# LSTM stage of a fused kernel: input rows added into the gate banks by TensorE, h split into three bf16 columns, no filler products

## The chip, the cores and the metric

The kernel runs on one core of a Trainium2 chip. The metric is the device time of one execution in microseconds (us), the median of three runs. TensorE is called PE, VectorE DVE, ScalarE ACT, GpSimd POOL and the DMA-issuing SyncE SP.

## The reference

The reference is a chain of eight layers over 625 rows of 512 features. Each adds its output to the rows. The change concerns the sixth, a recurrent cell chosen anew at each of 625 steps among four LSTM cells:

```python
def step(carry, x_t):
    h, c = carry
    logits = concatenate([h, c, x_t]) @ W_sel.T + b_sel
    onehot = one_hot(argmax(logits), 4)
    g_all = x_t @ W_ih[s] + h @ W_hh[s] + b_ih + b_hh        # for each cell s
    i, f, g, o = split(sum over s of g_all * onehot, 4)
    c2 = sigmoid(f) * c + sigmoid(i) * tanh(g)
    h2 = sigmoid(o) * tanh(c2)
    return (h2, c2), h2
```

Step 0 starts from c = 0 and uses cell 0. h, c and each gate have 512 elements. The 625 values of h are added to the rows.

## The kernel before

Eight stages run one after the other, each in blocks that end when every engine has ended. The function lstm has four such blocks, and the changed lines are all in them, save the host's layout of the constants (lay_out).

**lstm_inputs** (L1125) computes the input product of all steps and all four cells ahead of the recurrence. 64 tiles, one for each cell and each 128 of its 2,048 gate rows, take 4 f32 products (K = 128 each) of 313 and of 312 columns (L1218, L1220). ACT and DVE add the bias as they copy the tile out of PSUM (L1204, L1189), and POOL's queue stores 5 MB for each cell (L1174).

**split_weights** (L1257) loads the recurrent weights (4 loads of 4 MB), finds a power of two from their largest value, and writes each weight, times that scale, as two fp16 parts.

**lstm_steps** (L1334) is the recurrence: a loop on each engine, 624 times round. A state vector of 512 lies as 128 partitions of 4 columns. The order of one round is:

- PE adds the score of the four cells in one PSUM row: the input's part (L1434), c's part (L1437, 8 narrow f32 records), and tanh(c) against weights that were multiplied by the output gate (L1441, 8 records).
- DVE takes the largest score and its index (MAX8 L1524, FIND_INDEX8 L1526). PE reads the index into a register and branches to one of four bodies. DVE reads it too, and copies the input row of that step and cell out of a ring (L1530).
- The body, cell(s), has 96 products (L1456). h, as two fp16 columns (high part, rest) of a 128x32 stationary tile, is the operand that is loaded; the fp16 weights stream past it. Four products stand side by side in the array's columns (tile_position 0, 32, 64, 96). They come in three parts, each in its own PSUM bank: f (32 products of 128 columns), i and g together (32 of 256), o (32 of 128).
- DVE sums the 32 rows of each bank (add_rows, L1480), multiplies by the inverse scale and adds the input (add_input, L1486), and ACT applies sigmoid or tanh (L1406 to L1413). DVE makes f*c (L1492), i*g (L1497), c (L1503), the weighted score weights (L1507), h (L1513), h's high part (L1516) and h's rest (L1518). ACT makes tanh(c) (L1415). POOL copies h away (L1396).
- keep_clock_up (L1424) issues products of 128x128 by 512 columns into a bank that nobody reads: 3 after the score, 1 when h's rest is there, 4 after the body (L1427).

SP loads the ring of input rows, 25 steps at a time (L1379 to L1389).

**add_hidden** (L1572) turns the kept h and adds it to the rows.

Of the kernel before, what the change touches and what calls it, by code (L numbers as in the profile page):

```python
# [24 lines left out]
WARM_PICK, WARM_GATES = 4, 4  # L25
H_SCALE = 1024.0
# [1093 lines left out]
CHUNK = 25  # L1120
RING = 3 * CHUNK

def lstm_inputs(nc, ctx, B):  # L1125
# [7 lines left out]
    def sem(name):  # L1133
        return nc.alloc_semaphore("xg_" + name)

    (b_loaded, bias_ready, done, kept_a, kept_v, lx_done, lx_kept, lx_stored) = [sem(n) for n in (
        "b_loaded bias_ready done kept_a kept_v lx_done lx_kept lx_stored").split()]
    w_loaded = [sem(f"w_loaded{i}") for i in range(2)]
    stored = [sem(f"stored{i}") for i in range(2)]
    B.xg = nc.dram_tensor("lstm_xg", (CELLS, 128, STEPS * GC), F32, kind="Internal").ap()  # L1140
    B.lx = nc.dram_tensor("lstm_lx", (STEPS, CELLS), F32, kind="Internal").ap()
    xnT = B.xnT[:].rearrange("p (c n) -> p c n", c=KC)
    CUT = 313
    LOADS = 2 * CELLS
    with ExitStack() as here:
        w = sb("w", [128, 2, KC, GC // 2, 128], F32)
        b_ih = sb("b_ih", [128, CELLS * GC], F32)
        b_hh = sb("b_hh", [128, CELLS * GC], F32)
        ws = sb("ws", [128, KC, CELLS], F32)
        bs = sb("bs", [1, CELLS], F32)  # L1150
        g = sb("g", [128, 2, STEPS, GC], F32)
# [3 lines left out]
        @block.sync  # L1155
        def _(sp):
            sp.dma_start(b_ih[:], I["c_b_ih"]).then_inc(b_loaded, 16)
            sp.dma_start(b_hh[:], I["c_b_hh"]).then_inc(b_loaded, 16)
            sp.dma_start(ws[:], I["c_w_sel_x"]).then_inc(b_loaded, 16)
            sp.dma_start(bs[:], I["L2_ffn_b_sel"].rearrange("(a s) -> a s", a=1)).then_inc(b_loaded, 16)  # L1160
            for n in range(LOADS):
                if n >= 2:
                    sp.wait_ge(done, GC // 2 * (n - 1))
                sp.dma_start(w[:, n % 2], I["c_w_ih"][n // 2, :, :, n % 2]).then_inc(w_loaded[n % 2], 16)
            sp.wait_ge(lx_kept, 1)
            sp.dma_start(B.lx.rearrange("(j p) s -> p j s", p=R), lx[:]).then_inc(lx_stored, 16)
            sp.wait_ge(lx_stored, 16)

        @block.gpsimd
        def _(pool):  # L1170
            for s in range(CELLS):
                pool.wait_ge(kept_a, GC * (s + 1))
                pool.wait_ge(kept_v, GC * (s + 1))
                pool.dma_start(B.xg[s], g[:, s % 2].rearrange("p t g -> p (t g)")).then_inc(stored[s % 2], 16)  # L1174
            for i in range(2):
                pool.wait_ge(stored[i], 16 * (CELLS // 2))

        @block.vector
        def _(dve):
            dve.wait_ge(b_loaded, 64)  # L1180
            nc.vector.tensor_tensor(b_ih[:], b_ih[:], b_hh[:], ALU.add).then_inc(bias_ready, 1)
            dve.wait_ge(bias_ready, 1)
            for s in range(CELLS):
                if s >= 2:
                    dve.wait_ge(stored[s % 2], 16 * (s // 2))
                for c in range(GC):
                    i = s * GC + c
                    dve.wait_ge(done, i + 1)
                    nc.vector.tensor_scalar(g[:, s % 2, CUT:STEPS, c], B.bank[2 * (i % 4) + 1][:, 0:STEPS - CUT],  # L1189
                                            b_ih[:, i:i + 1], None, ALU.add).then_inc(kept_v, 1)  # L1190
            dve.wait_ge(lx_done, 1)
            nc.vector.tensor_copy(lx[:], B.bank[0][0:R, 0:NT * CELLS].rearrange("p (j s) -> p j s", j=NT)
                                  ).then_inc(lx_kept, 1)

        @block.scalar
        def _(act):
            act.wait_ge(bias_ready, 1)
            for s in range(CELLS):
                if s >= 2:
                    act.wait_ge(stored[s % 2], 16 * (s // 2))  # L1200
                for c in range(GC):
                    i = s * GC + c
                    act.wait_ge(done, i + 1)
                    nc.scalar.activation(g[:, s % 2, 0:CUT, c], B.bank[2 * (i % 4)][:, 0:CUT], ACT.Identity,  # L1204
                                         bias=b_ih[:, i:i + 1]).then_inc(kept_a, 1)

        @block.tensor
        def _(pe):
            for i in range(CELLS * GC):
                n = i // (GC // 2)  # L1210
                if i % (GC // 2) == 0:
                    pe.wait_ge(w_loaded[n % 2], 16 * (n // 2 + 1))
                if i >= 4:
                    pe.wait_ge(kept_a, i - 3)
                    pe.wait_ge(kept_v, i - 3)
                for c in range(KC):
                    wt = w[:, n % 2, c, i % (GC // 2), :]
                    nc.tensor.matmul(B.bank[2 * (i % 4)][:, 0:CUT], wt, xnT[:, c, 0:CUT], start=(c == 0),  # L1218
                                     stop=(c == KC - 1))
                    last = nc.tensor.matmul(B.bank[2 * (i % 4) + 1][:, 0:N - CUT], wt, xnT[:, c, CUT:N],  # L1220
                                            start=(c == 0), stop=(c == KC - 1))
                last.then_inc(done, 1)
            pe.wait_ge(b_loaded, 64)
            pe.wait_ge(kept_a, CELLS * GC)
            pe.wait_ge(kept_v, CELLS * GC)
            for m in range(NT):
                o = B.bank[0][0:R, m * CELLS:(m + 1) * CELLS]
# [11 lines left out]
def lstm(nc, ctx, B):  # L1239

    lstm_inputs(nc, ctx, B)
    with ExitStack() as here:
# [4 lines left out]
        L.raw = sb("w", [128, BLOCKS + SHIFT, 512], F32)  # L1247
        L.inv = sb("inv_scale", [128, 1], F32)
# [1069 lines left out]
```

## Time and profile before

| | |
|---|---|
| median of 3 runs | 6274.82 us (6270.7 to 6276.47) |
| the profiled execution | 6278.15 us |
| its span, first to last instruction | 6276.3 us |
| granted TensorE clock, mean of the span | 0.944 of full speed |
| PE busy | 5392.8 us (86%) |
| DVE busy | 3097.9 us (49%) |
| ACT busy | 1088.6 us (17%) |
| the recurrence's rounds | 2307.7 to about 5536 us |

Busy time of PE is modelled: a product of 512 fp16 columns counts some 0.38 us, of which the next one overlaps a part. A granted clock of 1.00 is 2.4 GHz, 0.50 is 1.2 GHz.

### The profile page before, as it was taken

The numbers are of one execution on the slowest core, as the hardware profiler recorded it, in microseconds if no ns is written. First come the engines' busy times: TensorE is split into PE (matmuls) and PEld (weight loads), VectorE is DVE, ScalarE is ACT, GpSimd is POOL, SyncE is SP. The second block draws the span as 40 slices with busy tenths as digits, with TensorE's granted clock in tenths as the row PEclk, the third lists the DMA queues.
The fourth block names the chain that finished last, engine by engine and source line by source line (L and its number), as shares of the span: only waits on it lengthen the run. The fifth ranks groups of instructions, "written<-read, shape, count | busy, mean of one in ns | idle before, by whom it ended". The sixth has DMA issues, their size and how long they took to land. (4 is left out here: it accounts for less than half of the span.)

```text
span 6276.3 us, 214043 instructions
## 1 busy us (share of the span) xinstructions
PE 5392.8 (86%) x84948; PEld 3269.5 (52%) x84948; DVE 3097.9 (49%) x13265; ACT 1088.6 (17%) x4645; POOL 612.9 (10%) x1014
## 2 busy tenths in 40 slices
PE   8998778849998929999999999999999999977778
PEld 6643443314666615555555555555555555544444
DVE  4401443214552165555555555555555555564543
ACT  0000000002331131111111111111111111122312
POOL 0000660002650000000000000000000000011100
PEclk9999998979999969999999999999999999989877
DMA  0000111467432330000000000000000000000010
GB/s 10 21 30 11 39 44 44 97 136 253 119 105 100 139 123 5 5 5 10 5 5 5 10 5 5 5 5 10 5 5 5 5 10 0 0 24 37 23 55 9
DMA packets 128787, 240.28 MB, mean 38 GB/s; under 512 B 47084, under 2 KB 64114, under 8 KB 127687
## 3 DMA queue, kind: packets, MB, share of 16 engines
q1 hardware_dynamic: 68584, 146.72, 6.6%
q0 software_dynamic: 60128, 92.58, 5.9%
q8 instruction: 45, 0.74, 0.0%
q14 instruction: 30, 0.25, 0.0%
HBM read 165.58 MB, written 73.29 MB: 38 GB/s over the span
## 5 line engine op out<-in xcount | busy, mean ns | idle before, releaser
L1456 PE MATMUL bank<-lstm_w,step_h_parts 128*32 128x128 f16 (+1 forms) x59904 | 1233.0, 238 | 172.1 <-issue 164.0
L1456 PEld LDWEIGHTS bank<-lstm_w,step_h_parts 128*32 128x32 f16 x59904 | 1116.8, 97 | 488.4 <-issue 478.0
L1427 PE MATMUL bank<-lstm_w 128*128 128x512 f16 x4992 | 1297.0, 383 | 3.2 <-issue 3.2
L1480 DVE TRANSPOSE_TENSOR_REDUCE step_summed<-bank 128x4 f32<-128x128 f32 x1872 | 670.0, 358 | 292.7 <-PE bank L1456 285.6
L1427 PEld LDWEIGHTS bank<-lstm_w 128*128 128x128 f16 x4992 | 386.4, 98 | 388.5 <-issue 5.1
L1406 ACT ACTIVATE step_act_out<-step_gates 128x4 f32<-128x4 f32 x625 | 128.5, 206 | 2082.3 <-DVE step_gates L1486 2078.8
L1486 DVE SCALAR_TENSOR_TENSOR step_gates<-step_summed,lstm_inv_scale,step_xgs 128x4 f32<-128x4 f32 x1872 | 416.0, 222 | 68.7
L1530 DVE COPY step_xgs<-step_xg 128x16 f32 x624 | 109.2, 175 | 688.7 <-issue 664.5
L1396 POOL COPY xnT<-step_state 128x4 f32 (+1 forms) x625 | 116.4, 186 | 3170.0 <-DVE step_state L1513 3170.0
L1109 PE MATMUL bank<-sum_parts,sum_hot 125*125 125x512 f16 x1600 | 347.6, 381 | 6.9 <-DVE sum_parts L1068 6.9
L1437 PE MATMUL bank<-lstm_wsel,step_state 128*1 128x4 f32 x4992 | 214.9, 168 | 115.3 <-DVE step_state L1503 115.3
L1109 PEld LDWEIGHTS bank<-sum_parts,sum_hot 125*125 125x125 f16 x1600 | 219.7, 137 | 135.1 <-DVE sum_parts L1068 7.8
L539 POOL DMA_INDIRECT gcn_rows<-gcn_h_rows,gcn_idx x160 | 202.5, 1266 | 704.4 <-issue 704.4
L1434 PEld LDWEIGHTS bank<-step_input_score,ones 1*1 1x1 f32 x1248 | 50.8, 76 | 380.4 <-issue 380.4
L1437 PEld LDWEIGHTS bank<-lstm_wsel,step_state 128*1 128x1 f32 x4992 | 147.1, 81 | 181.7 <-DVE step_state L1503 181.6
L227 PE MATMUL bank<-cnt_hot_s,cnt_hot_d 125*125 125x512 bf16 x800 | 222.2, 388 | 3.4 <-DVE cnt_hot_s L203 3.4
L1010 POOL DMA_INDIRECT sum_rows<-rel_h,sum_idx x160 | 212.1, 1326 | 118.3 <-DVE sum_idx L1063 80.3
L617 PE MATMUL bank<-gcn_hot,gcn_rows 125*128 125x500 f32 x320 | 177.9, 638 | 46.9 <-DMA gcn_rows<-gcn_h_rows,gcn_idx 43.0
L1434 PE MATMUL bank<-step_input_score,ones 1*1 1x4 f32 x1248 | 116.6, 161 | 115.9 <-ACT step_input_score L1411 115.9
L1441 PE MATMUL bank<-step_h_weight,step_tc 128*1 128x4 f32 x4992 | 214.2, 168 | 0.0
L944 PE MATMUL bank<-rel_zg,rel_mix 128*128 128x512 f32 x312 | 136.0, 599 | 76.8 <-DMA rel_z_last<-rel_z 76.8
L1218 PE MATMUL bank<-xnT,xg_w 128*128 128x313 f32 x512 | 178.2, 429 | 10.4 <-DMA xg_w<-in_c_w_ih 10.4
(368 smaller groups left out, 6578.2 us busy)
## 6 DMA issues: line engine op xcount, KB each, us to landing
rel_h<-rel_h_sb SPq DMA_DIRECT2D x39, 1024.0 KB, 4.3
lstm_xg<-xg_g POOLq DMA_DIRECT2D x4, 5000.0 KB, 19.5
step_xg<-lstm_xg SPq DMA_DIRECT2D x25, 800.0 KB, 4.4
xg_w<-in_c_w_ih SPq DMA_DIRECT2D x8, 2048.0 KB, 10.7
lstm_w<-in_c_w_hh SPq DMA_DIRECT2D x4, 4096.0 KB, 30.8
rel_z<-rel_z_sb POOLq DMA_DIRECT2D x8, 1250.0 KB, 22.9
rel_zg<-rel_z POOLq DMA_DIRECT2D x8, 1248.0 KB
cheb_w<-in_L_gnn_weight SPq DMA_DIRECT2D x8, 1024.0 KB
```

Of the source, the lines that this page charges most:

```text
L227: nc.tensor.matmul(B.bank[m][0:R, :], hd, hot_s[:, b, 0:512], start=False, stop=False)
L539: nc.gpsimd.indirect_dma_start(out=rows[:, i, :], out_offset=None, in_=h_dram, in_offset=bass.IndirectOffsetOnAxis(ap=idx[:, i:i + 1], axis=0)
L617: nc.tensor.matmul(B.bank[0][0:H, 0:500], rows[:, i, :], hot[:, i % 2, 0:500], start=False, stop=False)
L1010: nc.gpsimd.indirect_dma_start(out=rows[:, i, :], out_offset=None, in_=B.rel_h, in_offset=bass.IndirectOffsetOnAxis(ap=idx[:, i:i + 1], ax ...
L1109: last = nc.tensor.matmul(B.bank[m][0:R, :], hot[:, i % BUFS, m * R:(m + 1) * R], parts[:, i % BUFS, a, :], start=False, stop=False)
L1218: nc.tensor.matmul(B.bank[2 * (i % 4)][:, 0:CUT], wt, xnT[:, c, 0:CUT], start=(c == 0), stop=(c == KC - 1))
L1427: nc.tensor.matmul(idle[:], w[:, 0, 0, 0, 0, 0:128], w[:, 0, 0, 0, 0, :], start=True, stop=True)
L1437: nc.tensor.matmul(score[:, 0:CELLS], state[:, k:k + 1], L.wsel[:, :, k], start=False, stop=False)
L1441: last = nc.tensor.matmul(score[:, 0:CELLS], tc[:, k:k + 1], h_weight[:, :, k], start=False, stop=(k == KC - 1))
L1456: last = nc.tensor.matmul(bank[32 * q:32 * q + 32, 0:32 * (end - first)], h_parts[:, c, :], w[:, s, c, q, a, 32 * first:32 * end], start=( ...
L1480: nc.vector.tensor_reduce(summed[:, first:end], bank[:, 0:32 * (end - first)].rearrange("p (b r) -> p b r", r=32), X_AXIS, ALU.add, apply_ ...
L1486: nc.vector.scalar_tensor_tensor(out=gates[:, first:end], in0=summed[:, first:end], scalar=L.inv[:, 0:1], in1=xgs[:, first:end], op0=ALU.mult,
```

## The change

In the recurrence, the input rows are no longer copied and added by DVE. They lie in SBUF as bf16 rows: for each of the 16 pairs of gate and quarter three parts (high, middle, low), in 48 partitions, and the bias in another 48. One product for each gate (inject) with a constant 0/1 matrix as the loaded operand puts the rows of all four cells, 512 columns, into that gate's bank; the body then adds the recurrent product onto the 128 columns of the chosen cell. The gates are four parts now (f, g, i, o), each of 32 products of 128 columns. Injections of f and g stand at the head of PE's round, those of i and o after the score; keep_clock_up is gone. h is multiplied by the weights' inverse scale (a value in memory, in place of the constant 1024) and split in three bf16 columns; the split's second half (three DVE instructions) stands behind the choice of the cell. The add_input instructions are gone, and ACT reads the sums. lstm_inputs computes 80 tiles of 125 rows by 512 columns, splits them in three bf16 parts on ACT and DVE, and stores each tile by itself. The ring holds 15 steps in loads of 5.

```diff
@@ lstm_inputs
-                    nc.scalar.activation(g[:, s % 2, 0:CUT, c], B.bank[2 * (i % 4)][:, 0:CUT], ACT.Identity,
-                                         bias=b_ih[:, i:i + 1]).then_inc(kept_a, 1)
+                nc.scalar.copy(parts[:, i % 8, 0], B.bank[i % 6][0:R, :]).then_inc(hi_ready, 1)
+                nc.vector.tensor_tensor(rest[:, i % 4], B.bank[i % 6][0:R, :], parts[:, i % 8, 0], ALU.subtract
+                                        ).then_inc(rest_ready, 1)
+                nc.scalar.copy(parts[:, i % 8, 1], rest[:, i % 4]).then_inc(mid_ready, 1)
+                nc.vector.tensor_tensor(parts[:, i % 8, 2], rest[:, i % 4], parts[:, i % 8, 1], ALU.subtract
+                                        ).then_inc(lo_ready, 1)
+            for i in range(TILES):
+                n, m = i // NT, i % NT
+                pool.wait_ge(lo_ready, i + 1)
+                pool.dma_start(B.xg[n, :, m * R:(m + 1) * R, :].rearrange("a t g -> t a g"), parts[:, i % 8]
+                               ).then_inc(stored[i % 8], 16)
@@ lstm_steps, sync
+            sp.wait_ge(cleared, 1)
+            sp.dma_start(xg[64:64 + XG_ROWS, :, :], bias_rows.to_broadcast((XG_ROWS, XG_RING, 512))
+                         ).then_inc(bias_loaded, 16)
+                sp.wait_ge(injected, (k - (XG_SLOTS - 1)) * XG_CHUNK - 1)
+                load(k, k % XG_SLOTS)
@@ lstm_steps, tensor
-            def keep_clock_up(products):
-
-                for _ in range(products):
-                    nc.tensor.matmul(idle[:], w[:, 0, 0, 0, 0, 0:128], w[:, 0, 0, 0, 0, :], start=True, stop=True)
+            def inject(part, at, stop):
+                p, bank, _, _ = part
+                return nc.tensor.matmul(bank[:], rows[:, p, :], xg[:, at, :], start=True, stop=stop)
+
+            def add_half(part, s, c, a, stop):
+                p, bank, _, _ = part
+                for q in range(4):
+                    last = nc.tensor.matmul(bank[32 * q:32 * q + 32, 128 * s:128 * s + 128], h_parts[:, c, :],
+                                            w[:, s, c, q, a, 128 * p:128 * p + 128], start=False, stop=stop,
+                                            tile_position=(0, 32 * q))
+                return last
+
+            def cell(s):
+                for part in parts:
+                    for c, a in halves:
+                        last = add_half(part, s, c, a, stop=(c == KC - 1 and a == 1))
+                    last.then_inc(part[2], 1)
             with pe.Fori(1, STEPS) as t:
 
-                pe.wait_ge(init, 1)
-                pe.wait_ge(input_score_ready, t)
+                pe.wait_ge(xg_loaded, (t // XG_CHUNK + 1) * 16)
+                at = bass.ds(t % XG_RING, 1)
+                for part in (part_f, part_g):
+                    pe.wait_ge(part[3], t)
+                    inject(part, at, stop=False)
+                pe.wait_ge(input_score_ready, 1)
+                pe.sem_inc(input_score_ready, -1)
...
                 last.then_inc(score_done, 1)
-                keep_clock_up(WARM_PICK - 1)
-                pe.wait_ge(init, 1)
+                for part in (part_i, part_o):
+                    pe.wait_ge(part[3], t)
+                    last = inject(part, at, stop=False)
+                last.then_inc(injected, 1)
+                pe.wait_ge(picked, 1)
                 pe.wait_ge(h_lo_ready, t)
-                keep_clock_up(1)
-                pe.wait_ge(picked, 1)
                 s = pe.value_load(pick[0:1, 0:1])
...
-                keep_clock_up(WARM_GATES)
@@ lstm_steps, vector
-            def add_input(part, t):
+            def add_rows(part, s, n):
+                p, bank, done, summed_part = part
+                nc.vector.tensor_reduce(summed[:, 4 * p:4 * p + 4], bank[:, bass.ds(s * 128, 128)].rearrange(
+                    "p (b r) -> p b r", r=32), X_AXIS, ALU.add, apply_transpose=True
+                                        )._wait_ge(done, 1).then_inc(summed_part, 1)
...
-                nc.vector.scalar_tensor_tensor(out=state[:, 4:8], in0=act_out[:, 12:16], scalar=H_SCALE, in1=tc[:],
+                nc.vector.scalar_tensor_tensor(out=state[:, 4:8], in0=act_out[:, 12:16], scalar=L.inv[:, 0:1], in1=tc[:],
                                                op0=ALU.mult, op1=ALU.mult).then_inc(h_ready, 1)
                 dve.wait_ge(h_ready, n)
                 nc.vector.tensor_copy(h_parts[:, :, 0], state[:, 4:8]).then_inc(h_hi_ready, 1)
+
+            def split_h(n):
                 dve.wait_ge(h_hi_ready, n)
-                nc.vector.tensor_tensor(h_parts[:, :, 1], state[:, 4:8], h_parts[:, :, 0], ALU.subtract
+                nc.vector.tensor_tensor(h_rest[:], state[:, 4:8], h_parts[:, :, 0], ALU.subtract).then_inc(h_rest_ready, 1)
+                dve.wait_ge(h_rest_ready, n)
+                nc.vector.tensor_copy(h_parts[:, :, 1], h_rest[:]).then_inc(h_mid_ready, 1)
+                dve.wait_ge(h_mid_ready, n)
+                nc.vector.tensor_tensor(h_parts[:, :, 2], h_rest[:], h_parts[:, :, 1], ALU.subtract
                                         ).then_inc(h_lo_ready, 1)
...
                 nc.vector.max_index(pick[:], top[:], score).then_inc(picked, 1)
+                split_h(t)
                 dve.wait_ge(picked, 1)
                 s = dve.value_load(pick[0:1, 0:1], min_val=0, max_val=CELLS - 1)
-                dve.wait_ge(xg_loaded, (t // CHUNK + 1) * 16)
-                nc.vector.tensor_copy(xgs[:], xg[:, bass.ds(s, 1), bass.ds((t % RING) * GC, GC)]
-                                      ).then_inc(xgs_ready, 1)
                 dve.sem_inc(score_done, -1)
                 dve.sem_inc(top_ready, -1)
+                parts_taken()
+            with dve.Fori(1, STEPS) as t:
+                s = choose(t)
+                finish(s, t, t + 1)
```

parts_taken takes one off each of the four done semaphores. finish runs, in this order, the sums of f and g, f*c, the sums of i and o, i*g, c, the score weights, h and its high part. ACT runs f, g (tanh), i, the copy of the input score, o and tanh(c).

## Rows read from the trace of the kernel before

**Rows 1.** Windows: input block, recurrence. PE PEld DVE ACT POOL busy, PEclk, DMA.

```profile
1893.00:2185.00 292.00, 279.36 (x1066) 202.07 (x1066) 52.37 (x74) 55.08 (x69) 2.25 (x4) 0.97 0.29 113
...
2324.00:5535.00 3211.00, 2924.00 (x75885) 1857.94 (x75884) 1905.23 (x10574) 594.99 (x3732) 115.88 (x622) 1.00 0.02 6
```

**Rows 2.** Source L1524, the index search: duration, first and last start.

```profile
L1524 DVE MAX8 step_top<-bank x620: 160/163/164, 2330.5 to 5526.0; 1x8 f32<-1x8 f32 x155
```

**Rows 3.** Timeline of a round: start, us, instruction, [idle before it].

```profile
3502.39 1.95 PE L1456 MATMUL bank<-lstm_w,step_h_parts 128*32 128x128 f16 x96 [0.15 <-issue]
3502.84 0.17 DVE L1530 COPY step_xgs<-step_xg 128x16 f32 x1 [1.10 <-issue]
3503.41 0.32 DVE L1480 TRANSPOSE_TENSOR_REDUCE step_summed<-bank 128x4 f32<-128x128 f32 x1 [0.40 <-PE bank L1456]
...
3503.98 0.44 DVE L1480 TRANSPOSE_TENSOR_REDUCE step_summed<-bank 128x8 f32<-128x256 f32 x1
...
3504.27 1.04 PE L1427 MATMUL bank<-lstm_w 128*128 128x512 f16 x4
...
3504.60 0.31 DVE L1480 TRANSPOSE_TENSOR_REDUCE step_summed<-bank 128x4 f32<-128x128 f32 x1
...
3505.12 0.16 DVE L1497 TENSOR_TENSOR step_ig<-step_act_out 128x4 f32<-128x4 f32 x1 [0.21 <-ACT step_act_out L1409]
...
3505.41 0.16 DVE L1503 TENSOR_TENSOR step_state<-step_fc,step_ig 128x4 f32<-128x4 f32 x1
...
3505.85 0.16 DVE L1513 SCALAR_TENSOR_TENSOR step_state<-step_act_out,step_tc 128x4 f32<-128x4 f32 x1
...
3505.96 0.34 PE L1441 MATMUL bank<-step_h_weight,step_tc 128*1 128x4 f32 x8
3506.04 0.18 DVE L1516 CAST step_h_parts<-step_state 128x4 f16<-128x4 f32 x1
...
3506.26 0.18 DVE L1518 TENSOR_TENSOR step_h_parts<-step_state,step_h_parts 128x4 f16<-128x4 f32 x1
3506.34 0.16 DVE L1524 MAX8 step_top<-bank 1x8 f32<-1x8 f32 x1
...
3506.61 0.15 DVE L1526 FIND_INDEX8 step_pick<-step_top,bank 1x8 uint32<-1x8 f32 x1
...
3507.57 1.95 PE L1456 MATMUL bank<-lstm_w,step_h_parts 128*32 128x128 f16 x96 [0.30 <-issue]
```

**Rows 4.** Timeline, the last round: body and its first sum.

```profile
5532.63 1.95 PE L1456 MATMUL bank<-lstm_w,step_h_parts 128*32 128x128 f16 x96 [0.29 <-issue]
...
5533.33 0.32 DVE L1480 TRANSPOSE_TENSOR_REDUCE step_summed<-bank 128x4 f32<-128x128 f32 x1 [0.21 <-PE bank L1456]
```

**Rows 5.** Timeline, the first rounds.

```profile
2309.41 2.96 PE L1456 MATMUL bank<-lstm_w,step_h_parts 128*32 128x128 f16 x74
2310.51 0.32 DVE L1480 TRANSPOSE_TENSOR_REDUCE step_summed<-bank 128x4 f32<-128x128 f32 x1 [1.12 <-PE bank L1456]
...
2312.21 0.45 DVE L1480 TRANSPOSE_TENSOR_REDUCE step_summed<-bank 128x8 f32<-128x256 f32 x1 [1.05 <-PE bank L1456]
...
2316.31 1.89 PE L1427 MATMUL bank<-lstm_w 128*128 128x512 f16 x4 [3.24 <-issue]
```

**Rows 6.** Windows where the granted clock changed, columns as in rows 1.

```profile
2312.10:2315.50 3.40, 0.78 (x36) 0.43 (x26) 2.08 (x11) 0.73 (x5) 0.19 (x1) 1.00 0.55 202
2315.50:2319.00 3.50, 2.69 (x23) 1.09 (x24) 0.16 (x1) 0.00 (x0) 0.00 (x0) 0.51 0.02 5
5534.30:5537.70 3.40, 1.98 (x28) 1.18 (x16) 1.96 (x11) 0.67 (x4) 0.19 (x1) 1.00 0.00 0
5537.70:5541.10 3.40, 3.40 (x16) 3.40 (x16) 2.75 (x13) 0.00 (x0) 0.00 (x0) 0.50 0.01 2
```

**Rows 7.** Page, DMA issues: KB each, us to landing.

```profile
lstm_xg<-xg_g POOLq DMA_DIRECT2D x4, 5000.0 KB, 19.5
step_xg<-lstm_xg SPq DMA_DIRECT2D x25, 800.0 KB, 4.4
```

More of the change, by code:

```diff
@@ L1207, in _, with keep_mid @@
+            def keep_mid(i):
+                act.wait_ge(rest_ready, i + 1)
+                nc.scalar.copy(parts[:, i % 8, 1], rest[:, i % 4]).then_inc(mid_ready, 1)
+            for i in range(TILES + 1):
+                if i < TILES:
+                    keep_hi(i)
+                if i >= 1:
+                    keep_mid(i - 1)
         @block.tensor
         def _(pe):
-            for i in range(CELLS * GC):
-                n = i // (GC // 2)
-                if i % (GC // 2) == 0:
+            for i in range(TILES):
+                n, m = i // NT, i % NT
+                if m == 0:
@@ L1247, in lstm @@
         L.raw = sb("w", [128, BLOCKS + SHIFT, 512], F32)
+        L.scale = sb("scale", [128, 1], F32)
         L.inv = sb("inv_scale", [128, 1], F32)
@@ L1359, in lstm_steps @@
+    w = L.raw[:, 0:BLOCKS, :].bitcast(F16).rearrange("p (s c q) (a k) -> p s c q a k", s=CELLS, c=KC, a=2)
+    part_f = (0, B.bank[0], done_f, summed_f)
+    part_g = (1, B.bank[1], done_g, summed_g)
+    part_i = (2, B.bank[2], done_i, summed_i)
+    part_o = (3, B.bank[3], done_o, summed_o)
+    parts = (part_f, part_g, part_i, part_o)
+    score = B.bank[4][0:1, 0:8]
+    halves = [(c, a) for c in range(KC) for a in range(2)]
     with ExitStack() as here:
-        xg = sb("xg", [128, CELLS, RING * GC], F32)
@@ L1555, in _ @@
             dve.wait_ge(init, 1)
-            dve.wait_ge(xg_loaded, 16)
-            for first, end, _, _, _, gates_part in parts:
-                nc.vector.tensor_copy(gates[:, first:end], xg[:, 0, first:end]).then_inc(gates_part, 1)
-            forget(1)
-            new_i(1)
-            new_c(1)
-            weigh_h(1)
-            new_h(1)
-            choose(1)
-            with dve.Fori(1, STEPS - 1) as t:
-                finish(t, t + 1)
-                choose(t + 1)
-            finish(STEPS - 1, STEPS)
+            dve.wait_ge(rows_loaded, 16)
+            nc.vector.tensor_copy(rows[:], rows_f[:]).then_inc(rows_ready, 1)
+            finish(0, None, 1)
+            with dve.Fori(1, STEPS) as t:
+                s = choose(t)
+                finish(s, t, t + 1)
 def add_hidden(nc, ctx, B, L):
@@ L2290, in lay_out @@
         b = out.pop("L2_ffn_" + name).reshape(4, 4, 4, 4, 32)[:, order]
-        out["c_" + name] = np.ascontiguousarray(b.transpose(2, 4, 0, 1, 3).reshape(128, 64))
+        out["c_" + name] = np.ascontiguousarray(b.transpose(1, 2, 0, 3, 4).reshape(16, 512))
+    rows = np.zeros((128, 4, 128), np.float32)
+    for n in range(16):
+        rows[3 * n:3 * n + 3, n // 4, 32 * (n % 4)] = 1.0
+        rows[64 + 3 * n:64 + 3 * n + 3, n // 4, 32 * (n % 4)] = 1.0
+    out["c_xg_rows"] = rows
     w = out.pop("L2_ffn_W_sel")
```

252 lines of the change are left out of this document (125 added, 127 removed).

## The prediction

> **What bounds the kernel now.** I read the windows by stage first. The reader should see that the recurrence fills 3,211 of 6,276 us, that PE is busy 2,924 us of it at a granted clock of 1.00, and that the input block ahead of it is a PE stretch too, 279 of 292 us [rows 1]. The busy 91% is no proof that PE bounds the loop, because a good part of it is keep_clock_up. So the second view is the timeline of one round, read from instruction to instruction. The mean round is (5526.0 - 2330.5) / 619 = 5.16 us [rows 2]; the one that I take apart has 3507.57 - 3502.39 = 5.18 us [rows 3]. Counted from its first body product: the sum of f starts at 1.02, that of i and g at 1.59, that of o at 2.21 and it ends at 2.52; i*g starts at 2.73, c at 3.02 and ends at 3.18; the score's second half starts at 3.57, the largest score at 3.95, and the index is there at 4.37 (3506.61 + 0.15). The next body starts 0.81 later. Each of these waits for the one before it. The round is a chain of latencies over PE, DVE and ACT, and only what is on that chain has a price. The keep_clock_up products (1.04 us for four) start at 1.88, when the body is out, and lie beside the chain.
>
> **The gate part: a gain of 0.52 us a round.** The f sum starts at 1.02 inside the loop, but at 0.70 (5533.33 - 5532.63) in the last round, which stands behind the loop [rows 4]. The difference is DVE's register work: value load, input copy, decrements and loop end. The new loop has its loop end elsewhere, but four more decrements and the split ahead of this sum. From the index on, DVE now needs 3503.41 + 5.18 - 3506.76 = 1.8 us or less to its first sum; the split's dispatch adds some 0.4, and PE's product chain gives 0.60 + 0.81 + 0.70 = 2.1. The two are level; I take 0.70, and up to 1.0 would change nothing, because the o part decides. The body streams the same columns (32 x 128 four times for 32 x 128, 32 x 256, 32 x 128), so its 1.95 us stay. A consumer starts 0.04 after a product's modelled end (5.96 + 0.34 = 6.30, the search at 6.34 [rows 3]). So the o sum starts at 1.99 and ends at 2.30. No add_input and no late sigmoid stand between, since the i sum is finished before 2.0. i*g goes from 2.30 to 2.46, c from 2.50 to 2.66. Before it was 3.18: gain 0.52. Bounds: 0.40 (a semaphore step more) and 0.62 (i*g overlaps the sum's end).
>
> **The head of PE's round: a loss of 0.32.** The injections of f and g now stand ahead of the score on PE's queue, and behind the body, the loop's branch, and register work that PE did not do before (t over 5, t modulo 15, a computed operand address). keep_clock_up's products, which lay over the branch, are gone. No row shows this head. The nearest is DVE's 1.10 us of issue ahead of L1530, which has a value load in it [rows 3]; the bounds are 0 and 1.10, and I take 0.75, nearer to the upper end since the loop's branch is in it. The first injection then starts at 1.88 + 0.75 = 2.63. Four 512-column products take 1.04 us, the last one 0.38 of it by the page's model, so they follow each other at 0.22; two end their streaming at 3.07. The input's and c's score products take some 0.3 more, and the second half starts at 3.37. The chain would have been ready for it at 3.57 - 0.52 = 3.05. The loss is 0.32, with bounds 0 and 0.67. Queued behind the waiting injections is the whole score, and DVE's search waits for that. The injections of i and o come after the score and end 0.44 later, beside the search and the split: they cost nothing at full clock.
>
> **The split: a loss of 0.60.** Before, h's rest was made (6.26) ahead of the search, beside the score products. Now three dependent DVE instructions stand behind the index, and PE reads the index only after the last of them. h, its high part and its rest started 0.19 and 0.22 apart [rows 3], so three take 0.60 (bounds 0.48, three bare durations of 0.16, and 0.66). Everything of the next body is behind it. h with a scale from memory and DVE's loop end, now ahead of the search, cost 0 to 0.1; they hide in the 0.32 above, and cost that much if the head of PE's round is short.
>
> **Sum of the round at full clock:** 5.16 - 0.52 + 0.32 + 0.60 = 5.56 us, or +0.40. By the bounds it is between +0.08 (head hidden; 0.52 and 0.60 kept) and +0.75.
>
> **Around the loop: 0, give or take 10 us.** The input block streams 80 x 4 x 512 = 163,840 columns instead of 64 x 4 x 625 = 160,000: 2.4% of 272 us, +7. Its evictions (two ACT and two DVE passes a tile, in 3.4 us of PE time; now DVE and ACT are busy 52 and 55 of 292 us) and its 80 stores on POOL's queue hide behind PE; without that cover a store costs its landing, which no row shows at this size. The last store is 0.4 MB and not 5 MB (19.5 us to land [rows 7]), the first weight load 1 MB and not 2: some -10. The recurrence begins with a clearing of the ring, a bias load and a ring load in a row instead of a ring load alone (4.4 us [rows 7]): +5. SP issues 125 ring loads of 0.24 MB, each ten rounds (50 us) ahead against 4.4 us to land: nothing.
>
> **The clock: the largest term.** The filler streamed 8 x 0.22 = 1.7 us a round, the injections stream 0.9. Behind a body, PE then has 5.56 - 1.88 = 3.7 us with four injections (by the page's model two pairs of 0.60 = 1.2 us busy) and the four-column score products (some 0.7 busy). What the trace shows near that: in 2312.1 to 2315.5 PE was busy 0.78 of 3.40, and the clock was 0.51 in the next window; in 5534.3 to 5537.7 it was busy 1.98 of 3.40, with the last body's end, the four filler products and the first transposes, and the clock was 0.50 next. [rows 6] In the loop before, with both fillers in each round, it stayed at 1.00 for 3,200 us [rows 1]. I expect it to fall to 0.50 (1.2 GHz) in the stretch behind a body, again and again, and to come back only after a dense stretch, which is a slow body, so that it is high where PE has little to do. The price is in the first rounds: at half clock the sum of i and g started 2312.21 - 2309.41 = 2.80 after the body's start, at full clock 1.59 [rows 3, 5]. That is 1.21 for three quarters of the columns, and 1.61 for all. Four 512-column products take 1.89 instead of 1.04 us, 0.21 more each: 0.42 for the two injections ahead of the score [rows 5]. All at half clock: 5.56 + 1.61 + 0.42 = 7.59. I take two bodies in three and one injection pair in two: 1.07 + 0.21 = 1.28, a round of 6.84.
>
> The Trainium skill (TensorE: Matmul & The Clock Gate, "Why this matters for your kernels") says otherwise: throughput drops come from long PE-idle gaps between bursts of matmuls, and the gap it names is longer than any in this loop. By that rule alone the clock holds and the first rival below would be the result.
>
> **Rivals.**
> - *Forecast, chance 0.60: the clock falls.* 624 x (6.84 - 5.16) = 1,048; on the profiled execution's own 6,278 us that is 7,326, rounded to 7,330. Its own range: 6,800 (bodies at half clock in one round of three, a short head) to 7,800 (624 x 2.43 = 1,516, all at half clock).
> - *The clock holds, 0.27.* For it: the injections are full-width products, two before and two after the score, and the body still comes once a round. Against it: rows 6. 6,278 + 624 x 0.40 = 6,528, between 6,330 (+0.08) and 6,750 (+0.75).
> - *Faster, 0.06.* The place is the stretch from the body's last product to c. If c came over 0.60 us earlier, more than the split costs, with the head of PE's round hidden and the clock up, the kernel would gain; at 0.70 it is 6,278 - 624 x 0.10 = 6,216. For it: the f sum waits 0.3 us for DVE in the loop now. Against: I find 0.52 with the shortest steps of the rows.
> - *No change, 0.02:* the same, with gain and loss level.
> - *Instruction supply, 0.03.* A body is 128 products and loads for 96. In the first rounds PE stood 3.24 us on issue after its first body [rows 5] and never again. If the longer loop brought that back each round: +2,000 us, 8,300.
> - *The input block becomes bound by its stores, 0.02.* 31 MB in pieces of 1 KB instead of 20 MB. At double the 4.4 us per ring load of twice the size [rows 7], 80 stores take 350 us in place of 272: +80 on any of the above.
>
> **How the numbers follow.** The predicted time is the likeliest case's, 7,330. It stands to the median as the profiled execution does, 3 us above. Faster by over 0.2% 0.06, within 0.2% 0.02, slower 0.92; 0.2%, some 13 us, is about what a measurement of this kernel can tell from no change. The range takes in the rival with the clock up, from 6,400, and ends at 7,720: below lie faster and no change (0.08) and the low end of that rival (0.05), above it the instruction supply (0.03) and the top of the forecast (0.03).
>
> **What the profile would show.** The clock: windows over the recurrence with a granted clock well below 1.00 (I expect 0.6 to 0.8), and body records whose half-clock form is longer. Gate part: f sum 0.7 after the body's start and c some 0.6 after the o products' end. Head: the first injection 2.6 after the body's start, and the score's first half directly behind the second injection and not behind c. Split: three DVE instructions of 0.2 us between index and body, body start 1.4 us after the index (0.81 before). Wrong would be: a clock of 1.00, by which the forecast falls to the first rival; or a head under 0.4 us; or a DVE that reaches the f sum later than 1.0.

## The result, and the profile after

The change makes the kernel slower: 7190.6 us (median of 4 runs, 7185.69 to 7203.67) against 6274.57 us for the kernel before (median of 4 runs). The ratio is 1.1464, 95% interval 1.1444 to 1.1484. The profiled execution's span is 7190.4 us at a mean granted clock of 0.829 (0.944 before). The forecast was 7,330 us, in a range of 6,400 to 7,720, with the clock's fall as the likeliest case.

The page of the kernel after: engine busy time, the slices of PE, DVE and the clock, two groups (busy, mean ns of one | idle before).

```profile
PE 5496.8 (76%) x102037; PEld 3618.0 (50%) x102040; DVE 3056.5 (43%) x12745; ACT 1220.0 (17%) x4741; POOL 713.8 (10%) x1090
...
PE   9997878599992777777777777777777777767778
...
DVE  4303432145435444444444444444444444445543
...
PEclk9998989799995778777778777877777877778977
...
L1473 PE MATMUL bank<-lstm_w,step_h_parts 128*32 128x128 f16 x79872 | 1937.6, 285 | 869.6 <-DVE step_h_parts L1567 668.0
...
L1468 PE MATMUL bank<-step_xg,step_rows 128*128 (+1 forms) x2499 | 773.2, 392 | 351.7 <-issue 210.5
```

The clock row (PEclk, the granted clock in tenths of full speed) reads 7 to 8 in nearly every slice of the recurrence. Windows of the same trace, columns as in [rows 1]: the input block, 500 us of the recurrence, and two rounds cut in four.

```profile
1893.00:2185.00 292.00, 285.46 (x691) 128.73 (x691) 108.77 (x172) 91.28 (x165) 101.69 (x80) 0.98 0.56 161
...
3000.00:3500.00 500.00, 368.56 (x11229) 281.03 (x11228) 215.94 (x1192) 82.79 (x448) 13.78 (x74) 0.77 0.03 7
...
3503.40:3505.50 2.10, 1.97 (x128) 1.79 (x128) 1.07 (x5) 0.59 (x4) 0.00 (x0) 1.00 0.23 80
3505.50:3509.00 3.50, 1.73 (x22) 0.74 (x22) 1.82 (x12) 0.52 (x4) 0.19 (x1) 1.00 0.00 0
3509.00:3512.30 3.30, 3.26 (x129) 3.06 (x130) 0.99 (x4) 0.70 (x4) 0.00 (x0) 0.57 0.00 0
3512.30:3515.60 3.30, 1.97 (x22) 0.68 (x22) 1.90 (x12) 0.41 (x2) 0.19 (x1) 0.91 0.00 0
```

This is the pattern that the prediction described: one body at full clock, a stretch in which PE is busy 1.73 of 3.50 us, then a body of which most is at half clock (0.57), and behind it, where PE has little to do, a high clock again (0.91). The window ahead of the slow body still reads 1.00, so in this round the fall came only when that body had begun. The answers for the search (L1579) and the body's products (L1473) show how common it is (min/median/max ns, first and last start).

```profile
L1579 DVE MAX8 step_top<-bank x624: 161/163/164, 2312.9 to 6443.6; 1x8 f32<-1x8 f32 x156
```

```profile
L1473 PE MATMUL bank<-lstm_w,step_h_parts x79872: 219/314/315, 2315.1 to 6448.6; 128*32 128x128 f16 x200
```

The mean round is (6443.6 - 2312.9) / 623 = 6.63 us; the same count of the kernel before gives 5.17. A body product takes 219 ns at one level of the clock and 314 at the other, and the median is 314. With the page's mean of 285, (285 - 219) / (314 - 219) = 0.69 of them ran at half clock. I use this share for every run below. Counted by rounds in the same trace, 82 in 100 bodies (510 of 622) had products at half clock; a round with such a body took 6.85 us on average, one without 5.57.

The timeline of the round with the full-clock body, and the start of the next two bodies (start, us, instruction, [idle before]).

```profile
3503.40 1.97 PE L1473 MATMUL bank<-lstm_w,step_h_parts 128*32 128x128 f16 x128 [1.58 <-issue]
3504.08 0.76 DVE L1531 TRANSPOSE_TENSOR_REDUCE step_summed<-bank 128x4 f32 x2 [1.72 <-PE bank L1473]
...
3504.97 0.76 DVE L1531 TRANSPOSE_TENSOR_REDUCE step_summed<-bank 128x4 f32 x2
...
3505.66 0.12 DVE L1541 TENSOR_TENSOR step_ig<-step_act_out 128x4 f32<-128x4 f32 x1
...
3505.70 0.60 PE L1468 MATMUL bank<-step_xg,step_rows 128*128 x2 [0.34 <-DMA step_xg<-lstm_xg]
...
3505.81 0.16 DVE L1546 TENSOR_TENSOR step_state<-step_fc,step_ig 128x4 f32<-128x4 f32 x1
...
3506.55 0.34 PE L1506 MATMUL bank<-step_h_weight,step_tc 128*1 128x4 f32 x8
...
3507.05 0.16 DVE L1579 MAX8 step_top<-bank 1x8 f32<-1x8 f32 x1 [0.29 <-PE bank L1506]
...
3507.32 0.15 DVE L1581 FIND_INDEX8 step_pick<-step_top,bank 1x8 uint32<-1x8 f32 x1
...
3507.78 0.18 DVE L1567 TENSOR_TENSOR step_h_parts<-step_h_rest,step_h_parts 128x4 bf16<-128x4 f32 x1
...
3509.04 3.25 PE L1473 MATMUL bank<-lstm_w,step_h_parts 128*32 128x128 f16 x128 [1.61 <-issue]
...
3512.33 0.32 DVE L1531 TRANSPOSE_TENSOR_REDUCE step_summed<-bank 128x4 f32 x1 [0.54 <-PE bank L1473]
...
3513.96 0.16 DVE L1579 MAX8 step_top<-bank 1x8 f32<-1x8 f32 x1 [0.29 <-PE bank L1506]
...
3514.70 0.18 DVE L1567 TENSOR_TENSOR step_h_parts<-step_h_rest,step_h_parts 128x4 bf16<-128x4 f32 x1
...
3515.65 1.12 PE L1473 MATMUL bank<-lstm_w,step_h_parts 128*32 128x128 f16 x56 [1.38 <-DVE step_h_parts L1567]
```

Set against [rows 3], counted from the body's first product: the f sum at 0.68 (1.02 before), c at 2.41 (3.02), the score's second half at 3.15 (3.57), the largest score at 3.65 (3.95), the index there at 4.07 (4.37), but the next body at 5.64 (5.18). In the round after it the last sum ends at 3.61 and not at 2.33, and the search stands at 4.92 and not at 3.65: a body mostly at half clock costs 1.28 us here.

### The profile page after: what moved, and what is told of

It reads as the page before. It is cut to its first block and busy times, and to the rows that moved or that the text cites. A ratio compares the mean times of both kernels' runs of the same rounds, so it can differ in the third digit from the quotient of the medians.

```text
span 7190.4 us, 252028 instructions
## 1 busy us (share of the span) xinstructions
PE 5496.8 (76%) x102037; PEld 3618.0 (50%) x102040; DVE 3056.5 (43%) x12745; ACT 1220.0 (17%) x4741; POOL 713.8 (10%) x1090
## 5 line engine op out<-in xcount | busy, mean ns | idle before, releaser
L1473 PE MATMUL bank<-lstm_w,step_h_parts 128*32 128x128 f16 x79872 | 1937.6, 285 | 869.6 <-DVE step_h_parts L1567 668.0
L1473 PEld LDWEIGHTS bank<-lstm_w,step_h_parts 128*32 128x32 bf16 x79872 | 1824.3, 133 | 1175.9 <-issue 1175.9
L1531 DVE TRANSPOSE_TENSOR_REDUCE step_summed<-bank 128x4 f32 (+1 forms) x2500 | 791.9, 317 | 1919.9 <-PE bank L1473 1872.2
L1468 PE MATMUL bank<-step_xg,step_rows 128*128 (+1 forms) x2499 | 773.2, 392 | 351.7 <-issue 210.5
L1443 ACT ACTIVATE step_act_out<-step_summed 128x4 f32<-128x4 f32 x625 | 128.3, 205 | 2516.3 <-DVE step_summed L1531 2516.3
L1468 PEld LDWEIGHTS bank<-step_xg,step_rows 128*128 128x128 bf16 x2500 | 143.3, 98 | 488.3 <-issue 464.0
L1250 PE MATMUL bank<-xg_w,xnT 128*125 128x512 f32 x640 | 277.2, 596 | 5.9 <-DMA xg_w<-in_c_w_ih 5.9
L1250 PEld LDWEIGHTS bank<-xg_w,xnT 128*125 128x125 f32 x640 | 120.9, 189 | 161.7 <-issue 155.5
L1449 ACT ACTIVATE step_act_out<-step_summed 128x4 f32<-128x4 f32 x625 | 128.3, 205 | 359.0 <-DVE step_summed L1531 359.0
L1446 ACT ACTIVATE step_act_out<-step_summed 128x4 f32<-128x4 f32 x625 | 128.3, 205 | 356.2 <-DVE step_summed L1531 356.2
L1579 DVE MAX8 step_top<-bank 1x8 f32<-1x8 f32 x624 | 101.5, 163 | 203.5 <-PE bank L1506 203.5
```

What stands on the lines that cost most here:

```text
L1250: last = nc.tensor.matmul(B.bank[i % 6][0:R, :], xnT[:, c, m * R:(m + 1) * R], w[:, n % 2, c, :], start=(c == 0), stop=(c == KC - 1))
L1468: return nc.tensor.matmul(bank[:], rows[:, p, :], xg[:, at, :], start=True, stop=stop)
L1473: last = nc.tensor.matmul(bank[32 * q:32 * q + 32, 128 * s:128 * s + 128], h_parts[:, c, :], w[:, s, c, q, a, 128 * p:128 * p + 128], star ...
L1531: nc.vector.tensor_reduce(summed[:, 4 * p:4 * p + 4], bank[:, bass.ds(s * 128, 128)].rearrange("p (b r) -> p b r", r=32), X_AXIS, ALU.add, ...
```

## The experiments

Theory A: the clock makes most of the loss, and the rest is 0.40 us a round on the chain (a gain in the gate part, a loss at the head of PE's round and one by the split). Theory B: the clock is a sign and not a cause, and the chain itself is that much longer. Theory C, which came later: whether the clock falls depends on where the injections stand in the round. The expectations call the runs by the labels in the table.

| run (label) | median us | ratio to before, 95% interval | round us | mean body product ns | share at half clock |
|---|---|---|---|---|---|
| after | 7190.6 | 1.1464 (1.1444 to 1.1484) | 6.63 | 285 | 0.69 |
| 1 wide fillers (e1_fill4) | 6523.66 | 1.0397 (1.0367 to 1.0427) | 5.56 | 219 | 0 |
| 2 narrow fillers (e2_narrow) | 7107.14 | 1.1327 (1.1294 to 1.136) | 6.49 | 276 | 0.60 |
| 3 one wide filler (e8_fill1) | 6909.44 | 1.1007 (1.0987 to 1.1027) | 6.17 | 256 | 0.39 |
| 4 before, no fillers (e4_before_nofill) | 6980.97 | 1.1126 (1.1093 to 1.1158) | 6.31 | 328, of two widths | not worked out |
| 5 run 1, injections late (e3_inject_late) | 6461.35 | 1.0298 (1.0268 to 1.0328) | 5.47 | 219 | 0 |
| 6 run 5, DVE's loop turned (e5_loop_end) | 6282.89 | 1.0007 (0.9997 to 1.0017) | 5.17 | 219 | 0 |
| 7 run 6, h as a pair, 3+1 fillers (e6_pair) | 5977.28 | 0.9525 (0.9512 to 0.9538) | 4.69 | 219 | 0 |
| 8 the same, 1+1 (e7_pair_1_1) | 5975.48 | 0.9519 (0.9502 to 0.9537) | 4.68 | 219 | 0 |
| 9 the same, 0+1 (e10_pair_0_1) | 5969.54 | 0.951 (0.9482 to 0.9538) | 4.68 | 220 | 0.01 |
| 10 the same, none (e9_pair_0_0) | 5981.37 | 0.9529 (0.9501 to 0.9557) | 4.69 | 220 | 0.01 |
| 11 run 6, no fillers (e11_loop_end_nofill) | 6323.2 | 1.007 (1.0047 to 1.0092) | 5.24 | 224 | 0.05 |
| 12 run 10, f and g at the head (e12_pair_head) | 6234.36 | 0.9932 (0.9906 to 0.9957) | 5.10 | 230 | 0.12 |

The rounds are worked out from the first and last start of the search, as above.

**1. Four wide fillers put back.** Everything of the change stays; four 512-column products into an unused bank follow the second pair of injections.

```diff
                 last.then_inc(injected, 1)
+                keep_clock_up(4)
```

> The changed kernel with four filler products (128x128 by 512 columns, into a bank that nobody reads) after the injections of i and o, beside the index search and the split. If the clock is the cause of the long rounds, the granted clock stays at 1.00 and every round takes what a round with a full-clock body takes in the changed kernel's trace (5.64 us against 6.85 us): 7,190 minus 623 x (6.63 - 5.64), some 6,575 us. If the body is slow for another reason (bf16 beside fp16 operands, 256 instead of 192 instructions), the time stays near 7,190 us.

Measured 6523.66 us, 51 below the expected 6,575, which took the 5.64 us of one round for all. The rows of its trace, the body's products and the search:

```profile
L1478 PE MATMUL bank<-lstm_w,step_h_parts x79872: 216/219/230, 2312.6 to 5779.5; 128*32 128x128 f16 x200
```

```profile
L1585 DVE MAX8 step_top<-bank x624: 161/162/164, 2310.4 to 5775.9; 1x8 f32<-1x8 f32 x156
```

No body product is above 230 ns any more. Products whose result nobody reads, added to PE's work, took 667 us off the time. Theory B falls: the clock is a cause, worth 667 us, and the chain alone is worth (5775.9 - 2310.4) / 623 - 5.17 = 0.39 us a round.

**2. Thirty-two narrow products in the same place.** Each streams 4 columns. It asks whether it is PE's silence that lets the clock fall.

```diff
                 last.then_inc(injected, 1)
+                keep_clock_up(32, 4)
```

> The same place filled with 32 products of 4 columns: PE has no longer gap than with the four wide ones (32 x 0.025 = 0.8 us), but next to nothing streams. If long idle gaps between matmuls are what drops the clock, it holds as with the four wide fillers, some 6,575 us. If streamed columns are what counts, as the score's four-column products suggest, the clock falls as in the changed kernel and the time stays near 7,190 us.

Measured 7107.14 us. PE's timeline:

```profile
3505.39 0.60 PE L1473 MATMUL bank<-step_xg,step_rows 128*128 x2 [0.22 <-issue]
3505.93 0.19 PE L1504 MATMUL bank<-step_input_score,ones 1*1 1x4 f32 x2
3506.04 0.34 PE L1507 MATMUL bank<-lstm_wsel,step_state 128*1 128x4 f32 x8
3506.24 0.34 PE L1511 MATMUL bank<-step_h_weight,step_tc 128*1 128x4 f32 x8
3506.52 0.60 PE L1473 MATMUL bank<-step_xg,step_rows 128*128 x2
3506.96 0.94 PE L1468 MATMUL bank<-lstm_w 128*128 128x4 f16 x32
3508.81 3.37 PE L1478 MATMUL bank<-lstm_w,step_h_parts 128*32 128x128 f16 x128 [0.91 <-issue]
```

By the page's count PE is idle for only 0.91 us ahead of that body, and the body still takes 3.37. The narrow products (0.94 us for 32) win 83 us where the wide ones (1.03 us for four in run 1) win 667. That also answers a rival to run 1's reading: it is not enough that PE executes something in this place. In the timeline of the kernel after, the longest silence ahead of a body is 1.61 us. The Trainium skill (TensorE: Matmul & The Clock Gate, "Why this matters for your kernels") warns of long PE-idle gaps between bursts of matmuls; that avoiding them is enough is not borne out here. An earlier section of the same page of the Trainium skill ("A second HAM failure mode: psum-queue depth-cycling") tells of a kernel whose clock goes back and forth because PE idles briefly but often between groups of products. The trace agrees that the clock goes back and forth without a long gap, with 0.69 of the products at half clock; that the short idling is the cause here, no run shows.

**3. One wide filler instead of four.**

```diff
                 last.then_inc(injected, 1)
+                keep_clock_up(1)
```

> The changed kernel with one filler after the injections (four gave 6,524 us, none 7,191 us). If the clock depends on how much PE streams between two bodies, step by step, this lies between: fewer bodies at half clock than 81 in 100, 6,700 to 7,100 us. If any wide product at this place is enough, 6,520 us; if one changes nothing, 7,190 us.

Measured 6909.44 us, share 0.39: it lies in between. The clock is not lost or kept as a whole; some rounds keep it and others do not.

**4. The kernel before without its eight fillers.**

```diff
-WARM_PICK, WARM_GATES = 4, 4
+WARM_PICK, WARM_GATES = 0, 0
```

> The kernel before with all eight filler products of a round taken out, nothing else changed. Theory of the clock: it falls here too, most bodies run at half clock, 624 x 1.2 to 1.6 us more, 7,000 to 7,300 us. Rival: the fillers do nothing for the chain, 6,275 us or a little less.

Measured 6980.97 us, 19 below the expected range. Its window and one body:

```profile
3000.00:3500.00 500.00, 332.14 (x9002) 269.34 (x8998) 248.89 (x1344) 75.57 (x474) 14.72 (x79) 0.66 0.02 5
```

```profile
3504.85 3.51 PE L1455 MATMUL bank<-lstm_w,step_h_parts 128*32 128x128 f16 x96 [1.37 <-DVE step_pick L1525]
```

The granted clock is 0.66 where it was 1.00, and the body 3.51 us where it was 1.95 [rows 3]. In the kernel before, the fillers alone are worth 6980.97 - 6273.7 = 707 us. With run 1's 667 of the change's 7190.6 - 6274.6 = 916 us, this shows that most of the loss is the removal of keep_clock_up.

**5. All four injections after the score** (with run 1's fillers). The head of PE's round is then bare.

```diff
-                for part in (part_f, part_g):
-                    pe.wait_ge(part[3], t)
-                    inject(part, at, stop=False)
...
-                for part in (part_i, part_o):
+                for part in parts:
                     pe.wait_ge(part[3], t)
                     last = inject(part, at, stop=False)
```

> The first kernel of this call (four wide fillers) with all four injections after the score. My term for the head of PE's round said that the injections of f and g hold the score up by 0.32 us: then 624 x 0.2 to 0.3 less, 6,390 to 6,450 us. The rival: the index search waits for DVE's loop end as well (it starts 0.47 us after h's high part), and the time stays within 30 us of the first kernel, some 6,575 us.

Measured 6461.35 us: 62 us better than run 1, or 0.10 a round and not 0.32. That is less than the prediction's term asked for and more than the rival's 30 us. Two rows of its timeline point to the reason.

```profile
3500.84 0.34 PE L1508 MATMUL bank<-step_h_weight,step_tc 128*1 128x4 f32 x8
```

```profile
3501.53 0.16 DVE L1582 MAX8 step_top<-bank 1x8 f32<-1x8 f32 x1 [0.29 <-PE bank L1508]
```

The search starts 0.69 after the score's second half; before it was 3506.34 - 3505.96 = 0.38 [rows 3]. The search starts 0.31 us later than it has to for PE's sake. In the changed kernel DVE's loop end stands between h's high part and the search; in the kernel before it stood behind the search and the index, ahead of the gate sums. Run 6 tests whether that is the cause.

**6. DVE's loop turned**, so that its end falls between the split and the wait for the body, where DVE is idle anyway.

```diff
+            choose(1)
-            with dve.Fori(1, STEPS) as t:
-                s = choose(t)
+            with dve.Fori(1, STEPS - 1) as t:
+                s = take()
                 finish(s, t, t + 1)
+                choose(t + 1)
+            s = take()
+            finish(s, STEPS - 1, STEPS)
```

take holds what stood behind the split in choose: the value load and the decrements.

> As e3_inject_late, with DVE's loop turned so that it ends behind the split and no longer between h's high part and the search for the largest score. In e3 the search starts 0.35 us after the score's modelled end, where 0.04 is the least that rows show. Theory: DVE's loop end holds it up, and the round loses 0.3 us: 6,461 - 624 x 0.3, some 6,275 us. Rival: the loop end only moves ahead of the first gate sum, which then starts late by as much: within 40 us of 6,461.

Measured 6282.89 us, ratio 1.0007, against some 6,275 expected. The same two instructions:

```profile
3502.24 0.34 PE L1508 MATMUL bank<-step_h_weight,step_tc 128*1 128x4 f32 x8
...
3502.62 0.16 DVE L1582 MAX8 step_top<-bank 1x8 f32<-1x8 f32 x1
```

0.38 again. DVE's loop end was worth 5.47 - 5.17 = 0.30 us a round.

**7 to 10. h as an fp16 pair again**, made ahead of the search as in the kernel before. The 0/1 matrix of the injections holds the weights' scale times 1024 in place of 1, and ACT divides it out with a scale from memory. split_h is gone. The runs differ in how many fillers follow the body and the injections: 3 and 1 in run 7, 1 and 1, 0 and 1, none in run 10.

```diff
-        h_parts = sb("h_parts", [128, KC, 32], BF16)
+        h_parts = sb("h_parts", [128, KC, 32], F16)
...
-                nc.scalar.activation(act_out[:, 0:4], summed[:, 0:4], ACT.Sigmoid
+                nc.scalar.activation(act_out[:, 0:4], summed[:, 0:4], ACT.Sigmoid, scale=L.inv[:, 0:1]
...
                 dve.wait_ge(h_hi_ready, n)
+                nc.vector.tensor_tensor(h_parts[:, :, 1], state[:, 4:8], h_parts[:, :, 0], ALU.subtract
                                         ).then_inc(h_lo_ready, 1)
...
-                split_h(t)
...
+                keep_clock_up(3)
```

> As e5_loop_end, but h stays a pair of fp16 columns as in the kernel before (times 1024, both made ahead of the search), the constant matrix of the injections is multiplied by the weights' scale times 1024, and ACT multiplies by the inverse as it reads the sums. Fillers: one after the injections, three after the body. The term of the split (three DVE instructions between index and body, measured 0.5 us, and 0.2 us more from its end to the body) goes: 0.5 to 0.7 us a round less than e5, 5,830 to 5,960 us, under both kernels. Rival: a scale on ACT or the fillers after the body lie on the chain and give 0.3 back, some 6,100 us.

> e6_pair with one filler after the body instead of three: six wide products a round beside the body in place of eight, in a shorter round than any before. If that still keeps the clock, within 20 us of e6_pair; if not, bodies at half clock come back and the time is 200 us or more above e6_pair.

> e6_pair with only the filler after the injections, none after the body. One filler in the changed kernel at this place took the share of half-clock bodies from 81 to 42 in 100. In this shorter round I expect fewer still: 6,000 to 6,350 us; 5,975 us if five wide products a round are enough.

> e6_pair without any filler: the four injections and the body are all that streams, as in the changed kernel, in a round of 4.7 us at full clock. If the injections were enough for the clock in a shorter round, some 5,975 us as e6_pair and e7_pair_1_1. By the clock theory it falls: with half to eight tenths of the bodies at half clock, 1.6 us each, 6,450 to 6,800 us.

Measured 5977.28, 5975.48, 5969.54 and 5981.37 us: all are about 5% below the kernel before, and their intervals overlap. Run 7 was expected at 5,830 to 5,960 us and came out 17 above that. From run 6 to run 7 the split's removal, with ACT's scale and the moved fillers against it, brings 6282.89 - 5977.28 = 306 us, or 0.49 a round. That none of the fillers is needed any more was not expected: by the clock theory, run 10 was to take 6,450 us or more. PE's timeline in run 10:

```profile
3501.19 1.97 PE L1478 MATMUL bank<-lstm_w,step_h_parts 128*32 128x128 f16 x128 [0.49 <-issue]
3503.60 0.19 PE L1501 MATMUL bank<-step_input_score,ones 1*1 1x4 f32 x2 [0.44 <-PEq L1500]
3503.86 0.34 PE L1504 MATMUL bank<-lstm_wsel,step_state 128*1 128x4 f32 x8
3504.19 0.34 PE L1508 MATMUL bank<-step_h_weight,step_tc 128*1 128x4 f32 x8
3504.47 1.04 PE L1473 MATMUL bank<-step_xg,step_rows 128*128 x4
3505.86 0.35 PE L1478 MATMUL bank<-lstm_w,step_h_parts 128*32 128x128 f16 x12 [0.36 <-issue]
```

PE has the same four injections as in the kernel after, and the clock holds. Two things differ in what PE does: the round is shorter, and the injections stand together close to the next body. Runs 11 and 12 are meant to take these apart.

**11. Run 6 without fillers**: late injections, but the longer round with the split.

> e5_loop_end without its four fillers: four injections together after the score, as in e9_pair_0_0, where the clock held without fillers, but a round of 5.17 us at full clock instead of 4.67. If the stretch from one body to the next decides (3.4 us here, 2.9 in e9, 3.7 in the changed kernel), the clock falls and the time is 6,600 to 7,000 us. If it was the placing of the four injections together that held it, 6,280 us as with the fillers.

Measured 6323.2 us, only 40 over run 6; 0.05 of the products are at half clock. Of the two expectations, the one by the length of the stretch (6,600 us or more) failed, and the one by the injections' place is off by 40 us.

**12. Run 10 with the injections of f and g at the head**: the short round, but the change's places.

> e9_pair_0_0 with the injections of f and g back at the head of PE's round, as in the changed kernel. If the length of the stretch between two bodies decides, the clock holds here too and the time is that of e9 plus at most the 0.1 to 0.2 us a round that the head costs: 5,980 to 6,100 us. If the placing decides, it falls: over 6,400 us.

Measured 6234.36 us, 253 over run 10 and between what the two theories gave (up to 6,100 and over 6,400). PE's timeline:

```profile
3502.60 1.97 PE L1478 MATMUL bank<-lstm_w,step_h_parts 128*32 128x128 f16 x128 [0.72 <-issue]
3505.13 0.60 PE L1473 MATMUL bank<-step_xg,step_rows 128*128 x2 [0.56 <-issue]
...
3507.58 0.33 PE L1478 MATMUL bank<-lstm_w,step_h_parts 128*32 128x128 f16 x9 [0.72 <-issue]
```

The round with a full-clock body is 4.98 us against 3505.86 - 3501.19 = 4.67 in run 10. So 0.31 of the 0.41 a round is the head, which DVE's loop end no longer covers, and 0.10 is the clock.

Both seem to matter, then. With f and g at the head, the share at half clock is 0.69 in the long round (after) and 0.12 in the short one (run 12). With all four late it is 0.05 in run 11, though its full-clock round (5.17) is longer than run 12's (4.98). These kernels also differ in h's form and in DVE's loop, and the head itself makes the round longer, so the two are not cleanly apart. How they work together stays open; run 5 without fillers, the long round with late injections and nothing else, was not tried.

## Why the prediction was right

**The mechanism was right.** The clock is lost again and again around the end of the stretch behind a body, and it comes back with the slow body, so that it is high where PE has little to do: 1.00, 0.57, 0.91 in the windows above, 0.77 on average. Run 1, with run 2 as its control, shows it to be the cause. What the prediction did not have is that the injections' places and the round's length can keep the clock up without fillers (runs 10 to 12).

**The size, by the terms.**

| term, us a round | predicted | measured | from |
|---|---|---|---|
| gate part | -0.52 | -0.48, net (-0.61 at c) | before against run 7; the timeline |
| head of PE's round | +0.32 | +0.10 | runs 1 and 5 |
| DVE's loop end | 0 to 0.1 beside the head | +0.30 | runs 5 and 6 |
| split | +0.60 | +0.49, net | runs 6 and 7 |
| sum at full clock | +0.40 | +0.39 | run 1 |
| half clock: bodies, and injections | +1.07, +0.21 | +1.07 together | after against run 1 |

- *Gate part.* The f sum came at 0.68 (predicted 0.70) and the last sum ended at 2.33 (2.30). i*g started at 2.26, ahead of that end; the bound of 0.62 had named this overlap, and it is what happened. 0.61 is the gain at c. Over the round it comes to 5.17 - 4.69 = 0.48 in runs 7 to 10, where ACT's scale takes back some 0.05 (c at 2.46 and not at 2.41, last section).
- *Head.* The first injection came at 2.30 and not 2.63: 0.42 behind the body's 1.88, where I took 0.75. The second half of the score started at 3.15, not 3.37. The gain from this went to DVE's loop end: the search starts at 3.65 (3.37 + 0.38 = 3.75 by the prediction's steps). The two lie beside each other: removing the head alone gives 0.10, both 0.40, and with the loop end gone the head alone costs 0.31 (run 12). The prediction had the loop end at 0 to 0.1 once the head is short; it is 0.30. That term was mis-sized, and the search waits for it and not for the head.
- *Split.* The three instructions ended 3507.96 - 3507.47 = 0.49 behind the index (predicted 0.60). From there to the body it is 1.08 in one round and 0.77 in the next, where I took 0.81 for all. The step from index to body is 1.57 us in the one (5.64 - 4.07) and 1.26 in the other, around the 1.4 predicted.
- *Full clock.* The first rival's price was 6,528 us; run 1 gave 6523.66. Its fillers cost the chain nothing that can be seen: its mean round of 5.56 us is that of the kernel after where the body is at full clock (5.57). That the sum meets 0.39 so closely is in part luck: the gate part is 0.04 short, head and loop end together are 0.08 over and the split is 0.11 under.
- *The clock's price.* Predicted were two bodies in three at 1.61 us each, 1.07 a round, and 6.63 - 5.56 = 1.07 is measured. This too is in part luck: 82 in 100 bodies were slow, which is more, and a round with a slow body costs 6.85 - 5.57 = 1.28, which is less, because in part such a body still runs at full clock. The step that failed is "one injection pair in two": the injections' mean is 392 ns (L1468 above) against 385 on run 1's page, and 98 of the 2,499 took over 450 ns (run 1's row follows: median 387, longest 634). Hardly any ran at half, so the clock must mostly be back when the body ends. 624 x 0.21 = 131 us, which is nearly the whole of 7,330 - 7,191 = 139.

```profile
L1473 PE MATMUL bank<-step_xg,step_rows x2500: 379/387/634, 2307.1 to 5775.9; 128*128 x192, 128*128 128x512 bf16 x1
```

**Around the loop.** Run 1's span is 6521.6 - 6276.3 = 245 us longer, of which the rounds make 623 x 0.388 = 242: 3 are left, predicted 0 to 10. PE is busy 285 of the input block's 292 us, so its stores and evictions stayed hidden, and that rival is out. So is instruction supply, which would have added some 3 us to each round: in run 1 the mean round is 5.56 us. "Faster" asked for c over 0.60 earlier, the head hidden and the clock up; c was 0.61 earlier, but the clock fell, and DVE's loop end, in the head's place, was not hidden.

## What to carry to other kernels

Before you remove work that seems useless on an engine with time to spare, ask what it keeps up: here eight products a round that nobody reads were worth 707 us of 6274. Such an edit has its price where the engine's work is dense and would run slower, and the engine's idle share does not show it. When two things end side by side (PE's head and DVE's loop end), removing one shows little, here 0.10 us of 0.40. Turn a loop so that its end falls where the engine waits anyway, and keep the split of an operand where the chain waits for something else, here ahead of the search.

## What the runs showed that was not expected

- The clock can hold without fillers. In runs 10 and 11, with the four injections directly after the score, it nearly always did (shares 0.01 and 0.05); in the kernel after, with the same four in two pairs and a longer round, it did not (0.69).
- An ACT instruction with a scale from memory takes 297 ns for 128x4, one without it 206. The two rows are of the f gate's sigmoid, in run 10 and then in run 6:

```profile
L1443 ACT ACTIVATE step_act_out<-step_summed,lstm_inv_scale x625: 297/297/299, 2309.2 to 5235.3; 128x4 f32<-128x4 f32 x157
```

```profile
L1443 ACT ACTIVATE step_act_out<-step_summed x625: 205/206/207, 2311.6 to 5538.4; 128x4 f32<-128x4 f32 x157
```

  The Trainium skill (ScalarE: Activation LUTs, "What ACT_TABLE_LOAD costs") gives some 93 ns for each such operand, and the trace agrees with 91. On the path it is in part covered: c starts at 3503.65 - 3501.19 = 2.46 in run 10 and at 2.41 in run 6.
- 128 products that stream 128 columns each, with loads of 32 columns, take 1.97 us, as the 96 of the body before took 1.95 [rows 3] for the same columns.
